# Two cross-attention blocks: the first tile's scores around the last token scores, its maxima bank by bank, loads behind the turns, and ScalarE and VectorE one step sooner in each query

## What is computed

```
def _cross_attention(q_in, kv_in, wq, bq, wk, bk, wv, bv, wo, bo, bias_k, bias_v):
    qh = (q_in @ wq + bq).reshape(b, q_len, H, K)
    kh = (kv_in @ wk + bk).reshape(b, t, H, K)
    vh = (kv_in @ wv + bv).reshape(b, t, H, K)
    kh = jnp.concatenate([kh, jnp.broadcast_to(bias_k, (b, 1, H, K))], axis=1)
    vh = jnp.concatenate([vh, jnp.broadcast_to(bias_v, (b, 1, H, K))], axis=1)
    logits = jnp.einsum('bqhk,bthk->bhqt', qh, kh) / scale
    weights = jax.nn.softmax(logits, axis=-1)
    ctx = jnp.einsum('bhqt,bthk->bqhk', weights, vh).reshape(b, q_len, H * K)
    return ctx @ wo + bo
x = res + _cross_attention(_layer_norm(x, ...), xf, ...)
```

## Time and profile before

| | us |
|---|---|
| median of 3 runs | 1460.28 (1457.51 to 1460.68) |
| the profiled execution | 1458.31 |
| its span, first to last instruction | 1456.5 |
| TensorE busy | 1409.2 |
| VectorE busy | 983.2 |
| ScalarE busy | 869.1 |
| GpSimd busy | 486.1 |

### The profile page before, as it was taken

The page is one execution under the profiler, slowest core; times in us unless marked ns, Lnnn a source line. Parts: engine busy times, 40 slices in busy tenths (PEclk is TensorE's granted clock), DMA queues, the critical chain, the costliest instruction groups (busy, mean ns, idle before and its releaser), DMA issues.

```text
span 1456.5 us, 24705 instructions
## 1 busy us (share of the span) xinstructions
PE 1409.2 (97%) x9188; PEld 889.1 (61%) x9188; DVE 983.2 (68%) x2028; ACT 869.1 (60%) x1566; POOL 486.1 (33%) x393
## 2 busy tenths in 40 slices
PE   9999999999999999999999999999899999999987
PEld 5466666666666654566666666666554455555545
DVE  6856555555555658776566566565558998889886
ACT  6654554455455547645544544554445798889986
POOL 5546334334334200234523523530001433333300
PEclk9999999999999999999999999999999999999999
DMA  6399889889988831599988989887622799999998
GB/s 212 98 224 185 177 175 182 176 171 180 180 170 178 163 99 29 145 195 186 182 168 179 182 169 180 182 166 149 179 55 55 150 221 213 217 210 214 223 201 159
DMA packets 671059, 246.88 MB, mean 170 GB/s; under 512 B 643693, under 2 KB 645213, under 8 KB 670941
## 3 DMA queue, kind: packets, MB, share of 16 engines
q1 hardware_dynamic: 670940, 245.32, 83.1%
HBM read 85.28 MB, written 0.52 MB: 59 GB/s over the span
## 4 chain that ended last, share of the span: by engine, by line
PE 73%; DVE 8%; DMA 7%; ACT 6%; SPq 3%; issue 3%; ACTq 0%; DVEq 0%
PE SC L790 39%; PE PV L790 34%; DMA core<-qc 3%; DVE qc L1588 2%; ACT qc L1321 2%; DVE prob L1570 2%; DMA core<-core 1%; ACT prob L1312 1%; DVE core L1629 1%; ACT core L1305 1%; DMA qc<-core 1%; SPq L519 1%; DMA core<-in_wv_dram 1%; SPq L561 1%; ACT small L1329 1%
## 5 line engine op out<-in xcount | busy, mean ns | idle before, releaser
L790 PE MATMUL PV<-core 128*128 128x256 f16 (+1 forms) x4800 | 540.0, 270 | 16.1 <-DMA core<-core 6.1
L790 PEld LDWEIGHTS PV<-core 128*128 128x128 f16 x4800 | 458.9, 98 | 85.6 <-issue 13.9
L1253 ACT ACTIVATE prob<-SC,core 128x500 f32<-128x500 f32 x336 | 223.9, 674 | 413.9 <-DVE core L1594 413.9
L1563 DVE TENSOR_REDUCE mx<-SC 128x1 f32<-128x500 f32 x336 | 224.9, 670 | 327.5 <-PE SC L790 327.5
L790 PE MATMUL SC<-ctxT,qc 128*128 128x500 f16 x2016 | 443.7, 374 | 0.0
L790 PEld LDWEIGHTS SC<-ctxT,qc 128*128 128x128 f16 x2016 | 196.2, 97 | 206.5
L718 POOL CAST ctxT<-stage 128x750 f16<-128x750 f32 x64 | 69.1, 1079 | 438.6 <-PE SC L790 240.8
L1621 DVE SCALAR_TENSOR_TENSOR core<-prob,core 128x1500 f16<-128x1500 f32 x112 | 194.7, 1738 | 3.8 <-ACT core L1262 3.7
L1262 ACT ACTIVATE core<-prob 128x1500 f16<-128x1500 f32 x112 | 162.9, 1455 | 3.5
L790 PE MATMUL SC<-ctxT 128*128 128x512 f16 x552 | 132.0, 382 | 4.3 <-DVE core L1629 4.1
L790 PE MATMUL SC<-qc 128*128 128x512 f16 x480 | 114.8, 384 | 12.8 <-DVE mx L1570 12.8
(11 more groups left out here) (143 smaller groups left out, 1329.4 us busy)
## 6 DMA issues: line engine op xcount, KB each, us to landing
stage<-in_ctx_nat_dram SPq DMA_DIRECT2D x64, 384.0 KB, 3.9
stage<-in_ctx_t_dram SPq DMA_DIRECT2D x64, 375.0 KB, 3.4
stage<-in_ctx_p_dram SPq DMA_DIRECT2D x32, 384.0 KB, 3.9
core<-in_wq_dram SPq DMA_DIRECT2D x8, 512.0 KB, 3.6
core<-in_wk_dram SPq DMA_DIRECT2D x8, 512.0 KB, 3.6
core<-in_wv_dram SPq DMA_DIRECT2D x8, 512.0 KB, 5.5
core<-in_wo_dram SPq DMA_DIRECT2D x8, 512.0 KB, 5.1
core<-core SPq DMA_TRANSPOSE x224, 4.0
```

Of the source, the lines that this page charges most:

```text
L790: return nc.tensor.matmul(o, a, c, start=start, stop=stop, skip_group_check=skip)
L1253: nc.scalar.activation(prob[:, i, c * CW:c * CW + w], SETS[i][c][:, 0:w], ACT.Exp, bias=nmax[:, i, :], accum_out=sum3[:, i, c:c + 1]).then ...
L1563: nc.vector.tensor_reduce(mx3[:, t % 2, c:c + 1], SETS[t % 2][c][:, 0:w], AX_X, ALU.max)\
```

## The change

Six edits, made for both blocks:

1. Head 14's key products go to the PV banks, not TB, so heads 13, 14 and 15 use the same two banks in turn, and each waits for the one before (`qp_lo >= n - 1`).
2. The first tile's bank c = 2 comes first, before the token scores of heads 14 and 15; banks 0 and 1 come between head 14's key products and head 15's. The token column is a function of its own, behind head 15.
3. `first_maximum` on DVE takes the maximum of c = 2 without the token column (semaphore `early_scores`), then of banks 0 and 1, then copies the token's column, and reduces four numbers. It stands ahead of head 15's low key products, which TensorE now needs only at `weigh(l, 0)`.
4. ACT and DVE take query h + 1 ahead of the key products of head h - 1, where they took query h.
5. ACT loads the table for Exp ahead of head 15's key products, not behind them.
6. SP issues the next sample's pieces in steps 2 and 3 of the block's first sample (before: 1 and 2), and the weight chunks in steps 2 to 5 (before: 0 to 3).

```
-            if h == H - 2:
-                return TB[c]
-            return PV[c] if h % 2 else S[c]
+            return PV[c] if h % 2 or h == H - 2 else S[c]
...
             def loads(g, s):
-                if s in (1, 2) and g + 1 < 2 * B:
-                    for k in (2 * s - 2, 2 * s - 1):
+                first = 2 if g % B == 0 else 1
+                if s in (first, first + 1) and g + 1 < 2 * B:
+                    for k in (2 * (s - first), 2 * (s - first) + 1):
                         piece((g + 1) // B, (g + 1) % B, k, True)
...
-                        if x < 4:
-                            weights(W_O[l] + x, W_O[l] + x + 1)
+                        if 2 <= x < 6:
+                            weights(W_O[l] + x - 2, W_O[l] + x - 1)
...
-                        if n >= 4:
+                        if h >= H - 2:
+                            pe.wait_ge(qp_lo, n - 1)
+                        elif n >= 4:
                             pe.wait_ge(qp_lo, n - 3)
...
                     if h + 2 < H:
                         query(h + 2)
-                    if h >= H - 2:
-                        pe.wait_ge(qp_lo, DC * (H * l + H - 4) + h - (H - 2) + 1)
-                        scores(l, 0, h - (H - 2))
-                    if h == H - 2:
-                        pe.wait_ge(q_lo, H * (l + 1))
-                        token_score(h)
-                        token_score(h + 1)
-                    through_keys(h)
+                    if h < H - 2:
+                        through_keys(h)
+                pe.wait_ge(qp_lo, DC * (H * l + 3))
                 scores(l, 0, NB - 1)
+                pe.wait_ge(q_lo, H * (l + 1))
+                token_score(H - 2)
+                token_score(H - 1)
+                through_keys(H - 2)
+                for c in range(NB - 1):
+                    pe.wait_ge(qp_lo, DC * (H * l + H - 4) + c + 1)
+                    scores(l, 0, c)
+                through_keys(H - 1)
+                token_column(l, 0)
...
+            def token_column(l, x):
...
+                if x == 0:
+                    pe.wait_ge(max_part, 3 * TILES * l + 1)
+                if s == 0:
+                    pe.wait_ge(tokrow_full[par], 128 * l + 16 * (b - par) + 32)
+                ins = mm(bank[:, CW:CW + 1], tokrow[:, par, s * P:(s + 1) * P], one[:, :],
+                         False, True, skip=True)
+                ins.then_inc(score_ready, 1)
...
+                query_high(0)
                 for h in range(H + 1):
...
+                    if h + 1 < H:
+                        query_high(h + 1)
                     if h + 4 < 4 * WCH:
                         weights_high(2 * W_Q[l] + h + 4)
...
+                    if h == H:
+                        table(ACT.Exp)
...
-                table(ACT.Exp)
...
+                    if h == H:
+                        first_maximum(l)
...
+            def first_maximum(l):
...
+                t = TILES * l
+                dve.wait_ge(early_scores, l + 1)
+                nc.vector.tensor_reduce(mx3[:, 0, NB - 1:NB], SETS[0][NB - 1][:, 0:CW], AX_X, ALU.max).then_inc(max_part, 1)
+                for c in range(NB - 1):
+                    dve.wait_ge(score_ready, 3 * t + c + 1)
+                    nc.vector.tensor_reduce(mx3[:, 0, c:c + 1], SETS[0][c][:, 0:CW], AX_X, ALU.max).then_inc(max_part, 1)
+                dve.wait_ge(score_ready, 3 * t + NB)
+                nc.vector.tensor_copy(mx3[:, 0, NB:NB + 1], SETS[0][NB - 1][:, CW:CW + 1]).then_inc(token_max, 1)
...
+                nc.vector.tensor_reduce(nmax[:, 0, :], mx3[:, 0, 0:NB + 1], AX_X, ALU.max, negate=True)\
+                    .then_inc(negmax_ready, 1)
```

More of the change, by code:

```diff
@@ L302, in build @@
         max_part = sem("max_part")
+        early_scores = sem("early_scores")
+        token_max = sem("token_max")
         negmax_ready = sem("negmax_ready")
@@ L925, in scores @@
                             n += 1
[L926 to L931, removed]
+                    if c < NB - 1:
+                        ins.then_inc(score_ready, 1)
+                    elif x == 0:
+                        ins.then_inc(early_scores, 1)
+                    else:
+                        token_column(l, x)
+            def token_column(l, x):
+                b, s = divmod(x, RT)
+                par = b % 2
+                bank = SETS[(TILES * l + x) % 2][NB - 1]
+                if x == 0:
[4 more added lines that the diff above has]
+                         False, True, skip=True)
+                ins.then_inc(score_ready, 1)
             def weigh(l, x):
@@ L937, in weigh @@
                 i, par = t % 2, b % 2
+                if x == 0:
+                    pe.wait_ge(qp_lo, DC * H * (l + 1))
                 if s == 0:
@@ L1221, in query_projection, with query_high @@
             def query_projection(l):
-                for h in range(H + 1):
[L1223 to L1227, removed]
-                        nc.scalar.activation(hring[:, h % 4, 0, :], TB[h % 2][:, 0:NQ], ACT.Identity,
-                                             bias=col(("bq", l), h)).then_inc(q_hi, 1)
+                def query_high(h):
+                    act.wait_ge(q_mm, H * l + h + 1)
+                    if h >= 4:
+                        act.wait_ge(qp_mm, DC * (H * l + h - 3) + 1 - h % 2)
+                    nc.scalar.activation(hring[:, h % 4, 0, :], TB[h % 2][:, 0:NQ], ACT.Identity,
+                                         bias=col(("bq", l), h)).then_inc(q_hi, 1)
+                query_high(0)
+                for h in range(H + 1):
+                    if h + 1 < H:
+                        query_high(h + 1)
                     if h + 4 < 4 * WCH:
@@ L1469, in query_projection, with query_low @@
             def query_projection(l):
+                def query_low(h):
+                    head_low(h, TB[h % 2], q_hi, H * l + h + 1, col(("bq", l), h), q_lo)
+                query_low(0)
                 for h in range(H + 1):
-                    if h < H:
-                        head_low(h, TB[h % 2], q_hi, H * l + h + 1, col(("bq", l), h), q_lo)
+                    if h + 1 < H:
+                        query_low(h + 1)
                     if h + 4 < 4 * WCH:
@@ L1494, in query_projection @@
                                 ALU.mult, ALU.subtract).then_inc(qp_lo, 1)
+            def first_maximum(l):
[7 more added lines that the diff above has]
+                nc.vector.tensor_copy(mx3[:, 0, NB:NB + 1], SETS[0][NB - 1][:, CW:CW + 1]).then_inc(token_max, 1)
+                dve.wait_ge(max_part, 3 * t + NB)
+                dve.wait_ge(token_max, l + 1)
+                nc.vector.tensor_reduce(nmax[:, 0, :], mx3[:, 0, 0:NB + 1], AX_X, ALU.max, negate=True)\
+                    .then_inc(negmax_ready, 1)
             def bias_stream(name):
@@ L1659, in attention @@
                     g, t = B * l + b, TILES * l + x
-                    if x < TILES:
+                    if 0 < x < TILES:
                         maximum(t, 0)
@@ L1672, in attention @@
                             weights_low(2 * W_O[l] + i)
-                    if x < TILES and x not in (1, TILES - 1):
+                    if 0 < x < TILES and x not in (1, TILES - 1):
                         maximum(t, 1)
```

2 lines of the change are left out of this document (removed).

## The result

The changed kernel takes **1453.8 us** (median of 5 runs, 1452.15 to 1454.63) where the kernel before takes 1459.88 (5 runs): a ratio of 0.9957, 95% interval 0.9945 to 0.9969. The forecast was 1453.9. The profiled execution took 1454.63 us with a span of 1452.7, against 1458.31 and 1456.5. Of all executions that this document rests on, two were slow ones at a lower granted clock (one of e6, 2101.29 us at 0.65, and one of the kernel before beside e9 to e11, 1633.88 us at 0.85), and the ratios leave these two out.

A forecast was written before the change was run, and what follows sets the result against it. TensorE, 73% of the chain, bounds the kernel; its idle at both attention beginnings put 8.25 us at stake. Gains of 6.6 less 0.2 for loads give 6.4: 1460.28 - 6.4 = 1453.9, range 1451.3 to 1457.8.

The forecast's parts named there:

- 3.73 + 2.86: Gain at TensorE's weighings: tile 2 in block 0 starts 3.73 us sooner, tile 1 in block 1 2.86; sum 6.6.
- (a): TensorE's stop before the token scores of heads 14 and 15, waiting for DVE: 0.79 us lost in block 0, to go.
- (b): TensorE's stop at the token's column: 0.21 us lost in block 0, and that 0.21 of waiting was to stay.
- Exp: ACT's exp of tile 0, behind the first maximum, was to start at 61.28 us, not 62.97: 1.69 earlier.
- The copy: DVE's copy of the token's one column: taken as 0.16 us, up to 0.88 while POOL works beside it.
- The table load: ACT's Exp table load, 1.28 us, was to lie between heads 14's and 15's high key parts; uncovered, at most 1.28.
- The turns: Block 0: turn 0 issued at 64.88, landing 68.90, TensorE waiting 0.8 us; turn 1 landing at 72.7, 3.9 ahead of need.
- shifted by 534.17: Block 1 was to run block 0's chain 534.17 us later: tile 0's weighing at 603.07, tile 1's at 610.84.
- The loads: Chunks moved to later steps could delay turn 5, landing by 108.3 and wanted at 107.75: 0 to 0.6 us, taken 0.2.
- No later stage takes any back: The 6.4 us were to survive whole, since TensorE waits for nothing in following tiles and everything behind starts from its end.
- Queries don't stall: Answers the slower rival (0.04): new ACT and DVE order stalls query projection; at 0.35 us a head, 1463.
- the partial case: Rival (0.10): waits go only in part, loads hold turns 3 to 6 by 1 to 2 us; gain 2.9 to 5.

The follow-up runs named there:

- e6: Changed kernel with only the weight chunks put back in steps 0 to 3, pieces still in steps 2 and 3; 1454.24 us, ratio 0.9977 to the kernel before.
- e9: Changed kernel with, in block 1, the ctx_t piece that followed turn 0's transfers issued a step later; 1451.60 us, ratio 0.9963 to the kernel before.
- e11: Changed kernel itself, unedited, run again beside two edited versions; 1452.08 us, ratio 0.9962 to the kernel before.
- e5: Changed kernel with edit 4 undone, so ACT and DVE take query h again; 1455.12 us, ratio 0.9981 to the kernel before.
- e4: Changed kernel with edit 5 undone, Exp's table loaded behind head 15's high key parts; 1454.84 us, ratio 0.9977 to the kernel before.
- e8: Changed kernel once more, nothing edited; 1452.49 us, ratio 0.9965 to the kernel before.
- e7: Changed kernel with tile 3's scores ahead of tile 0's weighing in each block; 1452.86 us, ratio 0.9967 to the kernel before.
- e10: Changed kernel with tile 3's scores ahead of tile 0's weighing in both blocks, run once more; 1451.06 us, ratio 0.9958 to the kernel before.
- e3: Changed kernel with edit 3 undone, tile 0's maxima behind head 15's low key parts again; 1458.46 us, ratio 1.0001 to the kernel before.

## Why the prediction was right

- **The number.** The mechanism was right: 6.52 us by the distances, where 3.73 + 2.86 = 6.59 was forecast. That the median lies 0.1 us from the forecast is luck. The forecast stands on 1460.28, a median of three; the ratios of the three timings make 6.3, 5.1 and 5.5 us of the 6.4; and the profiled execution, for which the same working gave 1451.9, took 1454.63, since 3.0 us went where the working saw nothing.
- **Stops (a) and (b).** (a) is gone. Tile 1's scores begin 60.21 - 53.21 = 7.00 behind the first scores, forecast 60.31 - 53.49 = 6.82, before 7.61: 0.61 won of the 0.79. The token rows come 5.00 behind ScalarE's part of them, not 4.91. e5 shows that edit 4 does it.
- **Exp.** 60.97 - 53.21 = 7.76 against 7.79 (the working's own terms make the maximum ready at 61.28, not 61.25, which changes nothing). The copy took 0.15, its lower bound, though in block 1 one operation as small (L1658) took 1.21 beside GpSimd's split. The table load is covered, as the working said, but there edit 5 had no worth of its own, and without its cover the load was to cost at most 1.28 on parts that are due late. That term was mis-sized: e4 prices the edit at 2.0 us, because a load that stays behind head 15's products stands ahead of exp itself once edit 3 has taken the low parts off the path.
- **The turns.** Turn 0 is issued at 11.36 (forecast 11.39) and the weighing of tile 0 starts at 15.45 (15.41) from the first scores, waiting 0.67 (0.8). Turn 1 is issued at 15.50 (15.2) and lands 3.9 later. In block 1 the same turn, with no load ahead of it either, landed 5.8 behind its issue (5.9 in e8), still 2.0 before TensorE was there; the chain "shifted by 534.17" doesn't show why, and it stays open. Turn 2 landed in 4.4, where the text only asked that it not be late.
- **The loads.** The bound was 0 to 0.6, and the forecast took 0.2. Turn 5 is issued at 101.90, lands 5.5 later and holds the weighing by 0.03 at most (0.13 in e11): the next row of TensorE starts at 107.48, where 99.69 + 7.76 = 107.45 was possible. It landed as the working had it, with nothing to spare.
- **No later stage takes any back.** This held for everything the working named, and failed by 0.9 us for a dip in the clock that no row of before showed, and that all three profiles of the change have.
- **The rivals.** Queries don't stall: the eight heads in 22.35 to 42.93 show PE busy 20.58 and DVE 18.54, as the earlier trace rows. The waits at tiles 3 to 6 of the partial case did not come in the change's first profile, and of the other two only e8 has one, the 0.20 at tile 4; in e7 and e10, which have 0.8 less cover, turns 3 and 4 are the next late ones.

## What to carry to other kernels

When a chain of engines sets a stop, edits along it are not worth their own share: with the order on TensorE changed, one on VectorE was worth 4.6 us and a table load 2.0, in a change that won 6.5 in all. So ask of each edit what the path would be without it. A transfer that TensorE waits for should not stand behind loads that nobody needs yet on the same queue: one step more for such loads gave half of the gain. Compare small changes by distances between fixed points of the trace, here good to 0.25 us, where medians left 1.5 to 2 open, and take more than one profile of each kernel before a difference of a few tenths is called the edit's.

## What the runs showed of the hardware

- TensorE's clock fell to the lower level some 1 us after it had begun again behind 2.91 us of idle in one block, and did not behind 2.95 us in the other (e3); where it fell, 36 matmuls took 5.76 us for 4.09. It also fell at about 542 us in the changed kernel, where TensorE had stood idle for no more than 0.4 us at a time.
- VectorE and GpSimd on 128x1500 and 128x750 operands side by side: the later one is held, 1.71 to 2.59 or 1.51 to 3.04, and which of them it is turns on when a load lands (the cast behind the load began at 595.04 or 595.52). Held, VectorE's took 1.58 us and what was left of GpSimd's, in ten profiles.
- SyncE needs 1.4 us to issue a turn with nothing queued and more behind loads: 2.38 and 3.00 at 101.90 and 104.33 in the changed kernel.
